# Context attention with keys on partitions: scores made twice, sums from the values' product

## The reference, cut to what matters

```python
qkv = (x @ w_qkv.T).reshape(B, N, 3, H, D).transpose(2, 0, 3, 1, 4)
q, k, v = (qkv[0], qkv[1], qkv[2])
kv = context.reshape(B, N_c, 2, H, D).transpose(2, 0, 3, 1, 4)
extra_k, extra_v = (kv[0], kv[1])
k = jnp.concatenate([extra_k, k], axis=2)
v = jnp.concatenate([extra_v, v], axis=2)
attn = jnp.einsum('bhnd,bhmd->bhnm', q * scale, k).astype(jnp.float32)
attn = jax.nn.softmax(attn, axis=-1).astype(dtype)
out = jnp.einsum('bhnm,bhmd->bhnd', attn, v)
out = out.transpose(0, 2, 1, 3).reshape(B, N, C)
return out @ w_proj.T + b_proj
```

## Time and profile before

| | |
|---|---|
| median of 3 runs | 2659.5 us (2657.5 to 2660.42) |
| the profiled execution's own time | 2656.42 us |
| its span, first to last instruction | 2654.4 us |
| mean granted TensorE clock | 0.963 |
| context attention, first front matmul to last addition | 457.5 to 820.8 us |
| first scores of round 0, of round 63 | 465.37 us, 804.43 us |
| busy in the span: TensorE, VectorE, ScalarE, GpSimd | 2297.9, 1305.1, 990.5, 125.2 us |

### The profile page before, as it was taken

The page is one execution under the profiler, slowest core; times in us unless marked ns, Lnnn a source line. Parts: engine busy times, 40 slices in busy tenths (PEclk is TensorE's granted clock), DMA queues, the critical chain, the costliest instruction groups (busy, mean ns, idle before and its releaser), DMA issues. The chain is left out here.

```text
span 2654.4 us, 38037 instructions
## 1 busy us (share of the span) xinstructions
PE 2297.9 (87%) x14861; PEld 1640.4 (62%) x14861; DVE 1305.1 (49%) x2633; ACT 990.5 (37%) x2823; POOL 125.2 (5%) x193
## 2 busy tenths in 40 slices
PE   6778887899987999998999999997998988773884
PEld 4455655566655666666666666665886766662773
DVE  5456665777775344433544544465443545332003
ACT  3246554677773111111323333344222444323222
POOL 0000000000000000000000000003001000002003
PEclk8989999999999999999999999998999999997997
DMA  3000001000002000012000000000002000003332
GB/s 117 17 1 1 1 1 40 13 13 25 13 13 96 1 1 1 1 41 80 9 9 9 9 9 1 1 1 29 1 1 70 25 17 19 0 1 139 125 129 68
DMA packets 54767, 76.07 MB, mean 29 GB/s; under 512 B 8248, under 2 KB 42816, under 8 KB 53696
## 3 DMA queue, kind: packets, MB, share of 16 engines
q1 hardware_dynamic: 53056, 69.44, 7.8%
q0 software_dynamic: 1536, 4.20, 0.6%
HBM read 65.24 MB, written 8.39 MB: 28 GB/s over the span
## 5 line engine op out<-in xcount | busy, mean ns | idle before, releaser
L867 ACT ACTIVATE ca_prob<-bank,ca_nmax 128x512 f32<-128x512 f32 x256 | 174.0, 690 | 94.1 <-DVE ca_nmax L934 94.1
L934 DVE TENSOR_REDUCE ca_nmax<-bank 128x1 f32<-128x512 f32 x256 | 164.2, 684 | 56.0 <-PE bank L724 55.9
L867 ACT ACTIVATE na_prob<-bank,na_nmax 128x257 f32<-128x257 f32 x256 | 118.0, 474 | 192.3 <-DVE na_nmax L934 192.3
L1470 PE MATMUL bank<-XN,rf_W 128*128 128x512 f32 x384 | 170.9, 595 | 0.0
L1481 PE MATMUL bank<-rf_W,rf_h 128*128 128x256 f32 x768 | 170.8, 379 | 0.0
L1481 PEld LDWEIGHTS bank<-rf_W,rf_h 128*128 128x128 f32 x768 | 146.3, 190 | 32.7 <-issue 14.8
L738 PEld LDWEIGHTS bank<-cst,ca_prob 128*128 128x128 f32 x1024 | 112.4, 142 | 73.4 <-issue 63.4
L867 ACT ACTIVATE ra_prob<-bank,ra_nmax 128x256 f32<-128x256 f32 x256 | 118.1, 482 | 105.4 <-DVE ra_nmax L934 105.4
L1525 ACT ACTIVATE rf_r<-bank 128x512 f32<-128x512 f32 x96 | 57.3, 597 | 261.9 <-PE bank L1470 261.9
L738 PE MATMUL bank<-cst,ca_prob 128*128 128x128 f32 x1024 | 140.5, 280 | 6.6 <-DVE ca_pT L940 5.9
L934 DVE TENSOR_REDUCE na_nmax<-bank 128x1 f32<-128x257 f32 x256 | 90.9, 418 | 93.2 <-PE bank L724 93.2
(11 more groups left out here) (400 smaller groups left out, 4355.1 us busy)
## 6 DMA issues: line engine op xcount, KB each, us to landing
xl_w<-in_L_ffn_w SPq DMA_DIRECT2D x16, 1024.0 KB, 7.5
dp_cx<-in_ctx_tok SPq DMA_DIRECT2D x4, 1024.0 KB, 14.5
ca_v<-in_ctx_values SPq DMA_DIRECT2D x8, 512.0 KB, 4.7
rf_W<-in_L_ffn_w SPq DMA_DIRECT2D x8, 512.0 KB, 9.0
na_Wkv<-in_L_xattn_Wkv SPq DMA_DIRECT2D x1, 4096.0 KB, 16.1
na_cxT<-in_ctx SPq DMA_DIRECT2D x8, 512.0 KB, 3.3
ma_cxT<-in_ctx SPq DMA_DIRECT2D x8, 512.0 KB, 3.3
X<-in_x SPq DMA_DIRECT2D x1, 2048.0 KB, 7.8
```

What stands on the lines that cost most here:

```text
L867: e = act.activation(prob[:, n % 2, u, hh * keys:(hh + 1) * keys], S[u][:, hh * keys:(hh + 1) * keys], ACT.Exp, bias=nmax[:, n % 2, u, hh: ...
L934: v.tensor_reduce(nmax[:, n % 2, u], S[u][:, 0:W].rearrange("p (h k) -> p h k", h=per), AX.X, ALU.max, negate=True).then_inc(maxed, 1)
L1470: mm = pe.matmul(g.bank[n % 3][:], W1[:, k, c * P:(c + 1) * P], g.XN[:, k, gi * GT:(gi + 1) * GT], start=(k == 0), stop=(k == KD - 1))
```

## The change

The layer no longer calls attention_stream; a stream of its own, key_major_stream, takes its place. Its 64 iterations n have the same heads and queries, and 8 more drain it:

- Scores are made as before, but only for their maxima. VectorE writes the negated maximum of unit u into a column of Z; one transpose of Z for each iteration ("z") puts the maxima on a partition, and VectorE's shift_queries adds them to the queries, in a row of each head's 32 that was zero (qa).
- Scores are made a second time with keys on partitions ("turned"): the keys kf have a one in that row, so the product is score minus maximum. A turned unit is 2 matmuls of 128 keys x 256 queries, and ScalarE's exponential of it is what the product with the values reads (pT). The 16 transposes of a round, the copies to ca_pT and the sums along rows are gone.
- Sums come from the values' product: 16 features of each head's 32 columns of values are constant 0.25 instead of 0, so half of the rows of bank 7 hold the sums. Every 4 iterations ScalarE copies bank 7 to cp; 8 DMAs put the sums on partitions, VectorE inverts them, 8 DMAs put the inverses on 8 rows, and one matmul spreads them ("spread", 2 for each batch). GpSimd cuts the outputs out of cp (mask_outputs), VectorE multiplies.
- From the second batch on, the scores for maxima are 2 float32r matmuls in place of 1 float32 matmul, with queries and keys split into a rounded part and its rest (HalfStack). GpSimd makes the parts, and 24 DMAs for each batch move them to the other 16 partitions of each head.
- Scores and z share banks 0 to 2 in turn, turned units banks 3 to 5. The waits stand before each unit's matmul. A half iteration ("pair") issues two units' scores and two turned units of iteration n - 3, on the four row groups.

The option "stack" that attention_stream gets as well is used by no layer. Core of the diff:

```diff
+class HalfStack:
...
+        self.q_halves = sb("q_halves", [P, 2, 2, KD, 2, N], F32R)
+        self.k_halves = sb("k_halves", [P, 2, KD, 2, 2 * N], F32R)
+        self.k_rest = sb("k_rest", [P, KD, 2 * N], F32R)
...
+    def split_queries(self, po, b):
+        own = self.q[:, b % 2].unsqueeze(2).to_broadcast([P, KD, 2, N])
+        rounded, rest = self.q_halves[:, 0, b % 2], self.q_halves[:, 1, b % 2]
+        po.tensor_copy(rounded, own).then_inc(self.queries_split, 1)
+        po.wait_ge(self.queries_split, 2 * (b - 1) + 1)
+        po.tensor_tensor(rest, own, rounded, ALU.subtract).then_inc(self.queries_split, 1)
...
+    def split_keys(self, po, b, of):
+        k, rounded = self.keys[:, b % 2, :, of], self.k_halves[:, b % 2, :, :, of]
...
+        po.tensor_copy(rounded, k.unsqueeze(2).to_broadcast([P, KD, 2, N])).then_inc(self.keys_split, 1)
...
+        po.tensor_tensor(self.k_rest[:, :, of], k, rounded[:, :, 0], ALU.subtract).then_inc(self.keys_split, 1)
...
+    def move_queries(self, sp, b):
+        sp.wait_ge(self.queries_split, 2 * b)
...
+                    at, to = s + 16 * odd, s + 16 * (1 - odd)
+                    sp.dma_start(of[to:to + 16, :, odd].bitcast(F32), of[at:at + 16, :, odd].bitcast(F32))\
+                      .then_inc(self.queries_moved[b % 2], 16)
+    def move_keys(self, sp, b):
+        sp.wait_ge(self.keys_split, 4 * b)
...
+                sp.dma_start(self.k_halves[to:to + 16, b % 2, :, odd].bitcast(F32), self.k_rest[at:at + 16].bitcast(F32))\
+                  .then_inc(self.keys_moved[b % 2], 16)
+    def wait_stacked(self, pe, b):
+        pe.wait_ge(self.queries_moved[b % 2], 16 * 16 * ((b + 1) // 2))
+        pe.wait_ge(self.keys_moved[b % 2], 16 * 8 * ((b + 1) // 2))
...
+def key_major_stream(g, ctx, wl, n_weights, ld, load, front, front_at, qz, kk, vv, stack, project, finish):
...
+    events = []
+    for n in range(ITER):
+        events += [("s", n, u) for u in (0, 1) if n < NR]
+        events += [("z", n - 1)] if 1 <= n <= NR else []
+        events += [("s", n, u) for u in (2, 3) if n < NR]
+    at = {e: j for j, e in enumerate(events)}
+    def score_bank(e):
+        return g.bank[at[e] % 3]
...
+    TURN = (2, 3, 0, 1)
...
+    slots = []
+    for n in range(ITER):
+        b, r = divmod(n, R)
+        early, late = [], []
+        if n >= 10 and (n - 10) % 4 == 0 and (n - 10) // 4 < 2 * B:
+            early.append(("spread", (n - 10) // 4))
+        if n >= 15 and (n - 15) % R == 0:
+            early.append(("project", (n - 15) // R))
+        if b + 1 < B:
+            late += [("front", b + 1, k) for k in range(3) if front_at[k] == r]
+        slots.append([early, late])
...
+            for n in range(ITER):
+                b, r = divmod(n, R)
+                if n >= 7 and (n - 7) % 4 == 0 and (n - 7) // 4 < 2 * B:
+                    j = (n - 7) // 4
+                    sp.wait_ge(copied, j + 1)
...
+                    for odd in range(2):
+                        for a in range(4):
+                            h = 2 * a + odd
+                            sp.dma_start(sums[16 * h:16 * h + 16, j % 2],
+                                         cp[32 * a + 16 * (1 - odd):32 * a + 16 * (1 - odd) + 1, j % 2, odd])\
+                              .then_inc(sums_moved[j % 2], 16)
+                if n >= 8 and (n - 8) % 4 == 0 and (n - 8) // 4 < 2 * B:
+                    j = (n - 8) // 4
+                    sp.wait_ge(inverted, j + 1)
...
+                    for h in range(8):
+                        sp.dma_start(inv_rows[h:h + 1, j % 2], inv[16 * h:16 * h + 16, j % 2])\
+                          .then_inc(inv_moved[j % 2], 16)
+                if b + 1 < B:
+                    if r == 2:
+                        stack.move_queries(sp, b + 1)
+                    if r == 3 and b >= 1:
+                        sp.wait_ge(valued, R * b)
+                        sp.wait_ge(formed, 4 * b)
+                        if b >= 2:
+                            sp.wait_ge(stack.keys_split, 4 * (b - 1))
+                        load_batch(b + 1)
+                    if r == 6:
+                        stack.move_keys(sp, b + 1)
...
+            def form_keys(b, part):
+                of = slice(part * N, (part + 1) * N)
+                if part == 0:
...
+                for odd in range(2):
+                    keep = g.c("keep_one")
+                    po.tensor_scalar(kf[:, b % 2, :, odd, of], kk[:, b % 2, :, of], keep[:, 2 * odd:2 * odd + 1],
+                                     keep[:, 2 * odd + 1:2 * odd + 2], ALU.mult, ALU.add).then_inc(formed, 1)
...
+            def mask_outputs(j):
+                po.wait_ge(copied, j + 1)
...
+            for n in range(ITER):
+                b, r = divmod(n, R)
+                if b + 1 < B and r == 1:
+                    wait_freed(po, ("front", b + 1, 0))
...
+                    stack.split_queries(po, b + 1)
+                if n >= 8 and (n - 8) % 4 == 0 and (n - 8) // 4 < 2 * B:
+                    mask_outputs((n - 8) // 4)
+                if b + 1 < B and r == 4:
+                    form_keys(b + 1, 0)
+                    stack.split_keys(po, b + 1, slice(0, N))
+                if b + 1 < B and r == 5:
+                    form_keys(b + 1, 1)
+                    stack.split_keys(po, b + 1, slice(N, 2 * N))
...
+            def score(n, u, part, parts):
+                b, m, odd = quad(n // 2)
...
+                if part == 0 and at[e] >= 3:
+                    pe.wait_ge(taken, at[e] - 2)
...
+                    q = stack.q_halves[s:s + 32, part, b % 2, m, odd, i * P:(i + 1) * P]
+                    k = stack.k_halves[s:s + 32, b % 2, m, odd, :]
+                mm = pe.matmul(score_bank(e)[:], q, k, start=(part == 0), stop=(part == parts - 1), skip_group_check=True)
+                if part == parts - 1:
+                    mm.then_inc(scored, 1)
...
+            def turned_score(t, j, c):
...
+                    if pos >= 3:
+                        pe.wait_ge(exped, pos - 2)
+                    pe.wait_ge(taken, at[("z", 2 * (t // 2) + 1)] + 1)
+                tile = 2 * (t % 2) + c
+                mm = pe.matmul(g.bank[3 + pos % 3][:, c * N:(c + 1) * N],
+                               kf[32 * u:32 * u + 32, b % 2, m, odd, tile * P:(tile + 1) * P],
+                               qa[32 * u:32 * u + 32, odd], start=True, stop=True, skip_group_check=True)
...
+            def pair(n, first_unit):
+                t = n - 3
+                parts = 0 if n >= NR else 1 if n < R else 2
+                j0 = 0 if first_unit == 0 else 2
...
+                for step in range(2):
+                    if step < parts:
+                        for u in (first_unit, first_unit + 1):
+                            score(n, u, step, parts)
+                    if 0 <= t < NR:
+                        for j in (j0, j0 + 1):
+                            turned_score(t, j, step)
+            def turn_maxima(n):
+                e = ("z", n)
+                pe.wait_ge(taken, max(at[e] - 2, at[("s", n, 3)] + 1))
+                pe.transpose(score_bank(e)[:, 0:P], Z[:, (n // 2) % 2, n % 2], ident).then_inc(scored, 1)
...
+            def values(w):
+                b, m, odd = quad(w // 2)
+                pe.wait_ge(exped, 4 * (w + 1))
+                if w % 4 == 0 and w > 0:
+                    pe.wait_ge(copied, w // 4)
...
+                    pe.wait_ge(inv_moved[j % 2], 16 * 8 * (j // 2 + 1))
+                    mm = pe.matmul(bank[:, 0:N], g.c("head_row")[0:8, :], inv_rows[:, j % 2], start=True, stop=True)
...
+            for n in range(ITER):
+                pair(n, 0)
+                if 1 <= n <= NR:
+                    turn_maxima(n - 1)
+                for use in slots[n][0]:
+                    shared(use)
+                pair(n, 2)
+                if 0 <= n - 4 < NR:
+                    values(n - 4)
+                for use in slots[n][1]:
+                    shared(use)
...
+            def exps(t, j):
+                pos = 4 * t + j
+                act.wait_ge(t_ready, pos + 1)
...
+                act.activation(pT[:, t % 2, TURN[j]].rearrange("p c q -> p (c q)"), g.bank[3 + pos % 3][:], ACT.Exp)\
...
+                if n >= 7 and (n - 7) % 4 == 0 and (n - 7) // 4 < 2 * B:
+                    j = (n - 7) // 4
+                    act.wait_ge(valued, 4 * (j + 1))
...
+                    act.activation(cp[:, j % 2].rearrange("p o q -> p (o q)"), O[:], ACT.Copy).then_inc(copied, 1)
...
+                q = qz[:, odd, m] if b == 0 else stack.q[:, b % 2, m]
+                v.scalar_tensor_tensor(qa[:, odd, i * P:(i + 1) * P], q[:, i * P:(i + 1) * P], even01[:, odd:odd + 1],
+                                       score_bank(e)[:, 0:P], ALU.mult, ALU.add).then_inc(taken, 1)
...
+            for n in range(ITER):
+                if n < NR:
+                    maximum(n, 0)
+                    maximum(n, 1)
+                if 1 <= n <= NR:
```

(45 more changed lines are left out.)

258 lines of the change are left out of this document (242 added, 16 removed).

## The result

The changed kernel takes 2744.4 us (median of 4 runs, 2739.1 to 2748.8), the kernel before, measured beside it, 2658.5 us (2650.4 to 2660.4): ratio 1.0328, 95% interval 1.0298 to 1.0359. It is 86 us slower; the forecast was 12 us slower, and the range ended at 2715.

A forecast was written before the change was run, and what follows sets the result against it. The stage was taken as bound by the handing round between engines, with TensorE close behind. Stream -12.9, drain +21.3, slow clock +2.9 and constant load +0.3 gave +11.6 us, a forecast of 2671 us, range 2645 to 2715.

The forecast's parts named there:

- The new iteration, 4.27 us: An iteration of the new stream with float32r scores takes 4.27 us, where a round took 5.27 before.
- Late fronts: Three fronts for each batch, the next batch's projections, stand behind the values and add 1.73 us each.
- Side by side on the row groups: Forecast case: a half's scores and turned units run at once on TensorE, 1.07 us a half; 2671 us, chance 0.44.
- without overlap: Rival: float32r and float32 matmuls don't overlap on TensorE, turned scores stream after the scores; +48 us, 2719, chance 0.08.
- in strict order: Rival: a second record waiting for its group holds up all behind it, each half 0.22 later; +28, 2699, chance 0.08.
- the faster rival: Halves flow into each other, matmuls beginning once their own groups are free; 26 us less, 2645, chance 0.24.
- The 24 DMAs lie between the legs: On SP's queue HalfStack's moves fit between the DMAs of sums and inverses: queries moved by 19.1, next sums at 19.9.
- Stalls of 1.45 us a batch: In the stream, waits for the DMAs of sums and inverses cost 1.45 us per batch, 4.2 in the last.
- The clock: After the drain's idle gaps the clock is 0.50, so project and the next layer norm take 2.9 us more.
- legs 1 us longer: Rival: each run of DMAs for sums or inverses takes 1 us more, all exposed; +30 us, 2701, chance 0.16.
- The drain, 32.3: The drain after the stream, up to project's end, takes 32.3 us against 11.05 before, +21.3.
- The sign: Whole kernel: 11.6 us slower; chances 0.27 faster, 0.14 same, 0.59 slower.

The follow-up runs named there:

- e17: The changed kernel with its query moves issued by ScalarE's queue, three for each iteration, instead of SP's: 2753.8 us, ratio 1.0357.
- e1: The changed kernel with no sums moved or inverted, the spread reading constant ones, so the output stays undivided: 2678.6 us, ratio 1.0075.
- e4: The changed kernel without HalfStack: one float32 matmul for a unit's maxima in all batches, no splits and none of the 24 moves: 2716.7 us, ratio 1.0222.
- e11: e10 with one useless matmul in TensorE's gap before the second half where nothing else stands there: 2672.4 us, ratio 1.0053.
- e10: The changed kernel with sums turned by two float32 matmuls instead of DMAs, and half of the key moves on ScalarE's queue: 2688.2 us, ratio 1.0121.
- e2: The changed kernel with 7 useless float32 matmuls of 512 columns added in every fourth iteration: 2744.6 us, ratio 1.0328.
- e13: e11 with the fronts moved from behind values into TensorE's gap, and the reciprocal cut in two halves: 2640.1 us, ratio 0.9933.
- e18: e13 without its useless matmuls: 2646.6 us, ratio 0.9971.

## Why the prediction was wrong

- **The new iteration, 4.27 us:** right, 4.36 measured; +5 us over 55 iterations. Late fronts 1.93 (forecast 1.73), project 0.77 (1.0), so the undisturbed stretch is 6.7 us above its forecast.
- **Side by side on the row groups:** right. The rivals without overlap and in strict order fall by the rows at 679.84, and so does the faster rival: scores follow values 1.00 behind, as forecast, and a half takes 1.07. The rule that I had weighed, matmuls strictly in program order in start and end (the Trainium skill, TensorE: Matmul & The Clock Gate, "The mechanism" of Part 3), isn't borne out for records of different row groups by any run here. By the prediction's own working a half would have taken 0.22 us more in strict order, 1.29.
- **"The 24 DMAs lie between the legs":** wrong, the first step that failed. SP's pitch was taken from the earlier trace rows as 0.50 us; the moves took 0.64 to 0.70 each (10.2 to 11.2 us for 16 where 8 were forecast), the legs' issues 0.62 and more. The schedule had 0.8 us of slack at that place, 19.1 against 19.9, and the moves took 2 to 3 us more. The sentence that GpSimd or the moves might be late, and that each us would cost 7 in all, stood in the prediction, but without a chance of its own. The keys, forecast 1 to 2 us early, were 1.8 to 2.3 us late in four batches. e17 shows that the moves made the sums late: with the query moves out of SP's queue VectorE's longest wait fell from 5.4 to 3.1 us. e1 (-66) and e4 (-28 in spite of 22 us more work) show what the legs and the moves cost with all that follows, though neither separates the queue from the rest.
- **Stalls of 1.45 us a batch:** mis-sized. TensorE's waits come to some 21 us in iterations 9 to 64, where the forecast had 12.9 (6 x 1.45 + 4.2).
- **The clock:** the step that failed most. It was counted in the drain alone (+2.9), where TensorE has nothing for 5 us. Waits in the stream were priced at their own length. They measured 1.3 to 2.9 us, and at or behind nearly every one stand one to three stretches with a mean clock of 0.50 to 0.77, which cost some 47 us, and batch 0 some 5 more. The rival "legs 1 us longer" (2701) had the mechanism of the waits and not this price. e11 against e10 and e2 against the changed kernel show that the clock has a price of its own.
- **The drain, 32.3:** 39.7. The 32.3 had the project at full clock, and 1.7 us for its slow clock stood in the +2.9, so 34.0 compares with 39.7. The shape was right (two gaps, clock 0.50, project 3.75); legs measured 6.1 to 6.2 instead of 5.3 (four of them: +3.4), with the last values at half speed (3.64 us for 32 records) behind the first gap. The next layer norm began warm (2.05, not 3.22): 1.2 less.
- **The sign** was right by luck in the main. In the forecast the stream got 12.9 us shorter and the drain longer by more than that. The drain did (39.7 against 11.05), but the stream, from the first scores to the drain, got longer too: 399.9 us (465.15 to 865.00) against 344.3 before and 331.4 forecast.

By terms, in the profiled executions (2656.4 and 2739.1, +82.7): forecast +11.6, undisturbed iterations +6.7, waits +7.7, the clock behind them some +47, batch 0 +5, the drain +5.7, the next layer norm -1.2, other layers -2. That is some 80 us, and 2 to 3 stay open.

Where the gain went: e13 shows that the change's idea is worth 3.3 us a batch, once sums stay off the DMA queue, fronts stand in the gap and the clock holds. All of that hangs on moving the fronts (3 x 1.16 = 3.5 us a batch, 26 us in all), which is no part of the change; without it, e11 is 0.5% slower than the kernel before. I did not try the same in the kernel before. There a batch of eight takes 43.04 us with its fronts and eight rounds without one 8 x 5.27 = 42.2, so a better place could win at most some 0.9 us a batch there, and by this estimate e13 would keep 2.4 of its 3.3.

Open: outside of this layer the versions with sums turned inside are 4 to 14 us longer than the kernel before in their profiles (e13: 2637.5 - 363.2 = 2274.3, against 2654.4 - 383.8 = 2270.6), most of it in the last layer, whose clock in 120 us of its middle was 0.87 in e13 and 0.97 before. e4, which keeps the legs, shows 0.83 there. What sets it is not known.

## What to carry to other kernels

A wait in a stream that keeps TensorE nearly full can cost its own length and then more than that again in work at half clock (here 21 us of waits and some 47 behind them); price both, and look for the sum of length x (1 - granted clock) in the profile after. Small DMAs were cheap for the DMA engines (a share of 0.02 to 0.3 in most stretches above) and dear for the queue that issues them (0.62 to 0.74 us each): add up issue times for a whole period in order, and if two users meet with under a few us of slack, count on the meeting. Where a turn of a few rows is needed, two matmuls and a wider reciprocal added 1.0 to 1.5 us to an iteration here, where two legs of DMAs took 12 us from the copy to the spread; and shared work belongs in the gap that TensorE has anyway (a front added 1.93 us behind the values and 0.77 in the gap).

## What the runs showed of the hardware

- After a wait of 1.7 us the clock stayed at 0.50 for 50 us in e1 (780 to 830), and after one of 2.7 us for 47 us in e17 (about 825 to 872), with TensorE busy nearly all of it and the instruction mix that ran at 1.00 elsewhere. After another wait of such a size it came back much sooner: in the changed kernel at 709, 14 us after the wait of 2.94 us that ended at 694.83. What decides between the two is open.
- It also fell where TensorE's idle time in the whole iteration was 0.3 us (e17 after 589.99) or 0.7 us (e18 after 637.34), at places that differed from kernel to kernel.
- SP's pitch for small moves within SBUF was 0.62 us with nothing beside them (8 in 4.96 us, in the drain) and up to 0.74 in the stream (8 sums in 5.92 us at 636.16); loads from HBM were issued 0.51 to 0.52 apart (905.55 to 909.14 us). From issue to landing the moves took 1.7 us at 1 KB, 2.0 at 32 KB and 2.3 at 64 KB.
- A leg of 8 took 6.1 to 6.2 us from its first issue to the reciprocal or the matmul (865.76 to 871.89, 872.17 to 878.41).
